# A ring of four for kept edge rows, and four operands of an attention pass in PSUM

## What is computed

```python
x = _layernorm(x + gat(x))        # layer 0: two gat_conv, 4 heads of 32
x = _layernorm(x + neighbours(x)) # layer 1: weighted sum over edges, two branches
x = _layernorm(x + attention(x))  # layer 2: 8 heads of 16, then a feed-forward
x = _layernorm(x + edge_mlp(x))   # layer 3: per-edge MLP with two batchnorms, mean

# a gat_conv: softmax over the edges of a node, then a weighted sum
e = leaky_relu(alpha_s[src] + alpha_d[dst], 0.2)
e_exp = exp(e - segment_max(e, dst)[dst])
out = segment_sum(h[src] * (e_exp / denom[dst])[:, :, None], dst)

# layer 2: the score is a product of the node's query and the edge's key
w = einsum('ehd,ehd->eh', q[dst], k[src])

# layer 3
e = (x[dst] - x[src]) @ theta_w.T + x[src] @ phi_w.T
e = relu(bn(e, bn0_g, bn0_b)) @ fc1_w.T
e = relu(bn(e, bn1_g, bn1_b))     # bn needs sums over all edges first
x = relu(segment_sum(e, dst) / max(count, 1) + x)
```

## Time and profile before

| | us |
|---|---|
| median of 3 runs | 14954.79 |
| lowest and highest run | 14942.3, 14955.02 |
| the profiled execution | 14914.23 |
| its span | 14912.4 |
| busy in it: POOL, DVE | 8357.2, 7009.2 |
| busy in it: PE, ACT | 3867.0, 2521.3 |

### The profile page before, as it was taken

One profiled execution on the slowest core, in us unless ns is written; L12 is line 12 of the kernel. 1 busy time (PEld: TensorE's weight loads), 2 busy tenths in 40 slices (PEclk: granted clock), 3 DMA queues, 4 the chain that ended last, 5 costly groups with the idle time before them and its releaser, 6 DMA issues. The chain is left out here.

```text
span 14912.4 us, 95989 instructions
## 1 busy us (share of the span) xinstructions
PE 3867.0 (26%) x15751; PEld 2525.5 (17%) x15850; DVE 7009.2 (47%) x10781; ACT 2521.3 (17%) x6154; POOL 8357.2 (56%) x7838
## 2 busy tenths in 40 slices
PE   2011122223211222326920000000421111127666
PEld 1011011222211122223420000000211111113322
DVE  8673355556444555552034555555532222234454
ACT  0411122233212223320000000000000000004454
POOL 0116777777577777770017777777157777750012
PEclk9997565666655665657955555555655555558788
DMA  0002544444336434454703633333126433344444
GB/s 2 12 27 57 69 84 90 96 96 102 68 73 83 90 90 96 101 91 165 259 26 91 96 98 98 98 98 99 16 79 91 111 105 105 104 105 159 146 171 148
DMA packets 840654, 1414.44 MB, mean 95 GB/s; under 512 B 191956, under 2 KB 623802, under 8 KB 827672
## 3 DMA queue, kind: packets, MB, share of 16 engines
q0 software_dynamic: 277856, 659.70, 22.2%
q10 hardware_dynamic: 448192, 336.76, 8.3%
q1 hardware_dynamic: 114552, 417.44, 8.1%
HBM read 1058.01 MB, written 355.29 MB: 95 GB/s over the span
## 5 line engine op out<-in xcount | busy, mean ns | idle before, releaser
L851 POOL DMA_INDIRECT ring<-gat_table,index x3640 | 4056.4, 1114 | 1172.0 <-issue 1041.1
L851 POOL DMA_INDIRECT ring<-kv_table,index x1820 | 2030.2, 1115 | 577.8 <-issue 524.3
L851 POOL DMA_INDIRECT ring<-b_table,index x1820 | 1730.9, 951 | 670.0 <-issue 516.8
L982 PE MATMUL pairs<-hot_lo,hot_hi 128*128 128x128 f32 x6272 | 949.9, 325 | 1234.2 <-ACT hot_lo L1012 1232.7
L1076 DVE TENSOR_TENSOR prod<-ring,p 128x1848 f32<-128x1848 f32 (+1 forms) x390 | 820.3, 2103 | 721.7 <-DVEq L107 682.0
L982 PEld LDWEIGHTS pairs<-hot_lo,hot_hi 128*128 128x128 f32 x6272 | 923.7, 238 | 1287.4 <-issue 1285.9
L1012 ACT ACTIVATE hot_lo<-hot_lo,wt 128x128 f32<-128x128 f32 x3136 | 934.3, 387 | 1167.5 <-remote 1009.8
L1642 DVE TENSOR_TENSOR tb<-bt,att 128x1792 f32 x130 | 263.2, 2024 | 1663.7 <-DVEq L107 1663.7
L976 PE MATMUL pairs<-nil 128*128 128x512 bf16 x686 | 341.4, 596 | 2675.6 <-ACT dstage L1021 2629.6
L1125 ACT ACTIVATE p<-x 128x84 f32<-128x84 f32 (+1 forms) x390 | 114.2, 293 | 5220.4 <-DVE x L1072 5220.4
L1664 PE MATMUL bt<-ident,ring 128*128 128x128 f32 x1820 | 417.3, 421 | 1932.1 <-PEq L107 1932.1
(11 more groups left out here) (372 smaller groups left out, 8955.0 us busy)
## 6 DMA issues: line engine op xcount, KB each, us to landing
dense_weights<-dstage ACTq DMA_DIRECT2D x196, 1024.0 KB
mat<-dense_weights SPq DMA_DIRECT2D x98, 1568.0 KB
kept<-tb ACTq DMA_DIRECT2D x132, 896.0 KB, 3.8
layer_out<-kept SPq DMA_DIRECT2D x130, 896.0 KB
at<-kept SPq DMA_DIRECT2D x130, 896.0 KB
ring<-gat_table,index POOLq DMA_INDIRECT x3640
ring<-kv_table,index POOLq DMA_INDIRECT x1820
ring<-b_table,index POOLq DMA_INDIRECT x1820
```

The source lines that it names most:

```text
L851: pool.indirect_dma_start(self.ring[:, r * UG + i, :], None, self.table, bass.IndirectOffsetOnAxis(self.index[:, half, at:at + 1], 0)).the ...
L982: mm = pe.matmul(self.ps[:, b, i * P:(i + 1) * P], self.hot_hi[:, 4 * b + i, :], self.hot_lo[:, 4 * b + i, :], start=False, stop=False, sk ...
```

## The change

- In `attention_pass` the tile `prod` of 14 rows is replaced by `first` and `second` of 7 rows each, and its instruction by two, one for each edge. The kept share gets a tile `kept_share` of its own and an ACT instruction of its own. Where `beside` is None, which is layer 2, `p`, `first` and `acc` lie in PSUM; in layer 0 all of them stay in SBUF.
- The tile `qt` of layer 2 lies in PSUM.
- `KeptUnits` has its own ring `kept_ring` of `RU` = 4 units. SP issues two loads ahead of its loop and four in a round; ACT, PE and DVE take units 0 and 1 first and then four in a round. The tile `fold` of the spread pass lies in that ring, its `own` and `prod` in `layer_out`. Own batches stand before each of the first 7 rounds of four.

```diff
@@ -1038,9 +1038,12 @@
     with ExitStack() as st:
         s = k.sub(st)
         ga = Gather(k, s, table, width, slot_src)
-        e, x, p = (s.sb(n, [P, S + 1, HW]) for n in ("e", "x", "p"))
+        e, x = (s.sb(n, [P, S + 1, HW]) for n in ("e", "x"))
+        place = s.sb if beside is not None else s.ps
+        p, kept_share = place("p", [P, S, HW]), s.sb("kept_share", [P, HW])
+        first, second = place("first", [P, B7, VB]), s.sb("second", [P, B7, VB])
+        acc = place("acc", [P, B7, VB])
         warm = s.sb("warm", [P, 1])
-        prod, acc = s.sb("prod", [P, UG, VB]), s.sb("acc", [P, B7, VB])
         rden, newmax = s.sb("rden", [P, HW]), s.sb("newmax", [P, HW])
         work = extra(s)
         ch, e_ready, p_ready = (k.sem(n) for n in ("atchain", "e_ready", "p_ready"))
@@ -1073,21 +1076,24 @@
                                   ALU.subtract).then_inc(e_ready, 1)
                 claim(dve, p_ready)
                 weight = p[:, :, :].rearrange("p s (w h) -> p (s w) h", h=heads)
-                dve.tensor_tensor(by_head(prod[:, :, :]), by_head(got[:, :, 0:VB]),
-                                  weight[:, 0:UG, :].unsqueeze(3).broadcast_to([P, UG, heads, dim + 1]),
-                                  ALU.mult).then_inc(ga.used, 1)
+                share = kept_share[:, :].rearrange("p (w h) -> p w h", h=heads)
+                for half, dst in ((0, first), (1, second)):
+                    part = slice(half * B7, (half + 1) * B7)
+                    ins = dve.tensor_tensor(by_head(dst[:, :, :]), by_head(got[:, part, 0:VB]),
+                                            weight[:, part, :].unsqueeze(3).broadcast_to([P, B7, heads, dim + 1]),
+                                            ALU.mult)
+                ins.then_inc(ga.used, 1)
                 c(dve.tensor_tensor(by_head(acc[:, :, :]), by_head(acc[:, :, :]),
-                                    weight[:, UG:UG + B7, :].unsqueeze(3).broadcast_to([P, B7, heads, dim + 1]),
-                                    ALU.mult))
-                c(dve.tensor_tensor(prod[:, 0:B7, :], prod[:, 0:B7, :], prod[:, B7:UG, :], ALU.add))
-                dve.tensor_tensor(acc[:, :, :], acc[:, :, :], prod[:, 0:B7, :], ALU.add)
+                                    share.unsqueeze(3).broadcast_to([P, B7, heads, dim + 1]), ALU.mult))
+                c(dve.tensor_tensor(second[:, :, :], first[:, :, :], second[:, :, :], ALU.add))
+                dve.tensor_tensor(acc[:, :, :], acc[:, :, :], second[:, :, :], ALU.add)
                 c.reset()
 
             if rows_of is not None:
                 parts = Running(k, dve, EROWS)
                 parts.put(rows_of.chunks(dve, 0))
             with dve.Fori(0, NB) as b:
-                start(dve, c, b * B7, acc, e[:, S, :], work, prod)
+                start(dve, c, b * B7, acc, e[:, S, :], work, second)
                 c.reset()
                 u0 = band_start(k, dve, b)
                 if rows_of is None:
@@ -1122,7 +1128,8 @@
             def exponents(n):
                 with act.Fori(0, n):
                     take(act, e_ready)
-                    act.activation(p[:, :, :], x[:, :, :], ACT.Exp)
+                    act.activation(p[:, :, :], x[:, 0:S, :], ACT.Exp)
+                    act.activation(kept_share[:, :], x[:, S, :], ACT.Exp)
 
                     act.activation(e[:, S, :], newmax[:, :], ACT.Copy).then_inc(p_ready, 1)
 
@@ -1450,7 +1457,7 @@
                           lambda row: row[:, VB:2 * VB].rearrange("p (h c) -> p h c", h=H)[:, :, C:C + 1])
 
             stw.close()
-            qt = s1.sb("qt", [P, B7, VB])
+            qt = s1.ps("qt", [P, B7, VB])
             with ExitStack() as st2:
                 block = st2.enter_context(k.block())
 
@@ -1755,37 +1762,46 @@
 
 
 
-    def __init__(self, k, s, kept, coef, slots):
-        self.k, self.kept, self.coef, self.slots = k, kept, coef, slots
+    def __init__(self, k, s, kept, coef):
+        self.k, self.kept, self.coef = k, kept, coef
+        self.slots = s.sb("kept_ring", [P, RU, S * W7])
         self.r4 = s.sb("r4", [P, 2 * S, QW])
-        self.loaded = [k.sem(f"tb{h}_in") for h in range(2)]
+        self.loaded = [k.sem(f"tb{h}_in") for h in range(RU)]
         self.tb_free, self.r4_free, self.relued = k.sem("tb_free"), k.sem("r4_free"), k.sem("relued")
 
     def few(self, eng):
         return eng.If(pairs_of_units(self.k, eng) <= CAP // 2)
 
-    def pairs(self, eng):
-        return pairs_of_units(self.k, eng, CAP // 2)
+    def rounds(self, eng):
+        return eng.value_load(self.k.total[0:1, 1:2], min_val=NB + 1, max_val=CAP // RU)
 
     def prime(self, eng):
-        eng.sem_inc(self.tb_free, 2)
+        eng.sem_inc(self.tb_free, RU)
         eng.sem_inc(self.r4_free, 2 * S)
 
     def sync(self, sp):
+        def fetch(r, unit):
+            claim(sp, self.tb_free)
+            u = unit if isinstance(unit, int) else unit.with_bounds(min_val=0, max_val=CAP - 1)
+            sp.dma_start(self.slots[:, r, :], self.kept[ds(u, 1), :, :].rearrange("g p c -> (g p) c")
+                         ).then_inc(self.loaded[r], 16)
+
         with self.few(sp):
-            with sp.Fori(0, self.pairs(sp)) as i:
-                for h in range(2):
-                    claim(sp, self.tb_free)
-                    u = (2 * i + h).with_bounds(min_val=0, max_val=CAP - 1)
-                    sp.dma_start(self.slots[:, h * S * W7:(h + 1) * S * W7],
-                                 self.kept[ds(u, 1), :, :].rearrange("g p c -> (g p) c")).then_inc(self.loaded[h], 16)
-
-    def act_unit(self, act, h):
-        claim(act, self.loaded[h], 16)
+            for r in range(2):
+                fetch(r, r)
+            with sp.Fori(0, self.rounds(sp)) as i:
+                for r in range(RU):
+                    fetch((r + 2) % RU, RU * i + r + 2)
+
+    def act_units(self, act, slots):
+        for r in slots:
+            self.act_unit(act, r)
+
+    def act_unit(self, act, r):
+        claim(act, self.loaded[r], 16)
         for q in range(2 * S):
             claim(act, self.r4_free)
-            at = h * S * W7 + q * QW
-            act.activation(self.r4[:, q, :], self.slots[:, at:at + QW], ACT.Relu,
+            act.activation(self.r4[:, q, :], self.slots[:, r, q * QW:(q + 1) * QW], ACT.Relu,
                            bias=self.coef[:, 1:2], scale=self.coef[:, 0:1]).then_inc(self.relued, 1)
 
 
@@ -1795,9 +1811,10 @@
 
     with ExitStack() as st:
         s = k.sub(st)
-        source = KeptUnits(k, s, kept, coef, flat2(k.out[:, :, :]))
-        stats, fold = s.sb("stats", [P, CAP * 2 * S, 2, 3]), s.sb("fold", [P, CAP * 2 * S, 2])
-        own, prod = s.sb("own", [P, W7]), s.sb("prod", [P, W7])
+        source = KeptUnits(k, s, kept, coef)
+        stats = s.sb("stats", [P, CAP * 2 * S, 2, 3])
+        fold = flat2(source.slots[:, :, :])[:, 0:CAP * 4 * S].rearrange("p (g h) -> p g h", h=2)
+        own, prod = (flat2(k.out[:, i * B7:(i + 1) * B7, :]) for i in range(2))
         pad_sums = s.sb("pad_sums", [P, NB, 2])
         e1, d = s.ps("e1", [P, 2 * S, 512]), s.ps("d", [P, 2, 512])
         ch, product, bank_free, own_ready, own_free, d_done, d_free = (k.sem(n) for n in (
@@ -1810,18 +1827,17 @@
         def _(act):
...
@@ -1810,18 +1827,17 @@
         def _(act):
             def own_batch(b):
                 claim(act, own_free)
-                act.activation(own[:, :], at[:, ds(b * W7, W7)], ACT.Relu, bias=coef[:, 1:2],
+                act.activation(own, at[:, ds(b * W7, W7)], ACT.Relu, bias=coef[:, 1:2],
                                scale=coef[:, 0:1]).then_inc(own_ready, 1)
 
             with source.few(act):
-                last = source.pairs(act)
+                last = source.rounds(act)
+                source.act_units(act, (0, 1))
                 with act.Fori(0, NB) as b:
                     own_batch(b)
-                    source.act_unit(act, 0)
-                    source.act_unit(act, 1)
+                    source.act_units(act, (2, 3, 0, 1))
                 with act.Fori(NB, last):
-                    source.act_unit(act, 0)
-                    source.act_unit(act, 1)
+                    source.act_units(act, (2, 3, 0, 1))
 
         @block.tensor
         def _(pe):
...
-                last = source.pairs(dve)
+                last = source.rounds(dve)
                 source.prime(dve)
                 dve.sem_inc(bank_free, 2 * S)
                 dve.sem_inc(own_free, 1)
                 dve.sem_inc(d_free, 1)
                 c(dve.memset(stats[:, :, :, :], 0.0))
                 c.reset()
+                for u in range(2):
+                    unit(u)
                 with dve.Fori(0, NB) as i:
                     own_batch(i)
-                    unit(2 * i)
-                    unit(2 * i + 1)
+                    for u in range(RU):
+                        unit(RU * i + u + 2)
                 with dve.Fori(NB, last) as i:
-                    unit(2 * i)
```

(11 more changed lines are left out.)

24 lines of the change are left out of this document (14 added, 10 removed).

## The result

The changed kernel takes 13918.24 us (median of 4 runs, 13916.23 to 13925.74), beside 14948.55 for the kernel before on the same chip (4 runs, 14920.12 to 14955.02): a ratio of 0.9315, 95% interval 0.9299 to 0.9331. I had forecast 13815, with 13720 to 13980 as the range. The profiled execution took 13925.74 us with a span of 13923.9; before it was 14912.4. Between these two executions lie 988.5 us, where I had forecast 1138; between the medians lie 1030. So a difference of some 20 us between kernels of two sets is within that spread, and is read from the profiles.

What follows compares the result with a forecast made beforehand. POOL's gathers, held by DVE instructions with two SBUF inputs, bound the attention passes; two load places bound the kept passes. 299 + 229 + 327 + 283 = 1138 us off 14914 gives 13776, as median about 13815, range 13720 to 13980.

Steps and rivals of the forecast that it cites:

- Layer 2: Layer-2 attention: with one PSUM input in the wide DVE instructions, gathers are no longer held; 299 us less, range 256 to 310.
- Rivals (3): Layer-2 attention: PSUM inputs don't free the gathers, because it is not the port; nothing gained there, 14114 us; chance 0.05.
- (4): Layer-2 attention: PSUM operands make DVE the bound and the kernel slower than before, 15090 us; chance 0.01.
- Layer 0: Layer-0 attention: stalls stay, but the divided product holds gathers for less time; 229 us less, bounds nothing to 593.
- 260 units x 0.88 us: Layer-0 attention: the third gather begins at 3012.56 instead of 3013.44, a saving taken for every unit; 229 us.
- Rival (2): Layer-0 attention: the halves hold the port as one, so nothing is gained there; 14044 us; chance 0.07.
- Spread pass: First kept pass: four places make PE the bound at 0.75 us a product; 440 us against 767, 327 less.
- Mean pass: Second kept pass: DVE the bound at 0.77 us a product; 453 us against 736, 283 less.
- lead 5: Mean pass: 5 us counted before the products, within its sum of 453 us.
- 0.5 us of slow clock each: Mean pass: added to `dve_rows`' 7.6 us at each of six changes of band, 48 us together.
- Rivals (1): Kept passes gain only part: overlapping loads slow one another or PE's clock stays low; 14075 us (0.12), in full 14425.
- (5): Kept passes: the ring does nothing, SP's loads being served one at a time; 14425 us; chance 0.02, shared with (1) in full.

Runs made afterwards that it cites:

- the two edits: Changed kernel with layer 0's five wide instructions each cut into 4 + 3 tiles of nodes and empty slots reading 128 dummy rows: 13519.39 us.
- ring alone: Kernel before with only the changes to `KeptUnits` and its users, the ring of four for kept rows: 14377.99 us, ratio 0.962.
- empty slots: Changed kernel with 128 dummy rows in each table, an empty slot of partition i reading the i-th: 13729.81 us, ratio 0.9196.
- the query alone: Changed kernel with the tile `qt` back in SBUF instead of PSUM: 14094.66 us, ratio 0.9429.

## Why the mean pass gained less

After's mean pass has 20.9 us before its first product (forecast 5), 428.0 us for 520 products, 0.823 each (forecast 0.77), and six gaps for `dve_rows` of 7.5 us or less, 43.7 together (forecast 48 with the slow clock).

**The lead** is in the timeline of its start:

```profile
13396.25 28.89 SPq L1786 DMA_DIRECT2D kept_ring<-kept  x6
13401.00 2.72 ACT L1804 ACTIVATE r<-kept_ring,coef 128x448 f32<-128x448 f32 x4 [9.29 <-ACTq L107]
13406.19 3.37 POOL L2107 TENSOR_SCALAR lift<-ext,coef,bound 128x896 f32<-128x896 f32 x1 [518.55 <-issue]
...
13414.43 2.07 POOL L2110 TENSOR_TENSOR acc<-acc,lift 128x896 f32<-128x896 f32 x1
...
13417.11 1.27 DVE L2103 SCALAR_TENSOR_TENSOR acc<-e,bound,acc 128x448 f32<-128x448 f32 x2 [22.40 <-DVEq L107]
```

ACT has its four quarters at 13403.7. DVE waits until POOL has worked out the first band's start value, at 13416.5. So I moved these four instructions to DVE, on top of the two edits:

```diff
+                    tail.first_init(dve, c)
...
-                    tail.pool_init(pool, c, 0, 0)
```

> As the kernel with both edits, and the first band's start value of the mean pass (four instructions over 896 columns) on DVE, which waits for it, instead of on POOL. In the profile of after POOL begins them at 13406.19, 10 us behind the first load, and DVE's first product waits until 13417.11. On DVE they take about 4.5 us and can begin at about 13395. If POOL's start value sets the pass's lead, DVE's first product comes some 7 us behind the first load rather than 20.9, and the time falls by 10 to 14 us, which is under what the median can tell but plain in the profile. If PE's first product (13405) or the cold TensorE clock sets it, the lead stays above 15 us.

Measured: 13498.85 us (13496.27 to 13506.28), 0.9036 [0.9023, 0.9048], 20 less than with the two edits. Its start:

```profile
12991.95 2.73 SPq L1798 DMA_DIRECT2D kept_ring<-kept  x4
12992.30 0.75 DVE L2127 TENSOR_SCALAR layer_out<-ext,coef,bound 128x896 f32<-128x896 f32 x1 [1.90 <-issue]
...
12994.93 1.09 DVE L2130 TENSOR_TENSOR acc<-acc,layer_out 128x896 f32<-128x896 f32 x1
...
13000.06 0.68 DVE L2115 SCALAR_TENSOR_TENSOR acc<-e,bound,acc 128x448 f32<-128x448 f32 x1 [4.03 <-DVEq L107]
```

The first product comes 8.1 us behind the first load instead of 20.4: 12 us, as the theory has it. The other 8 us are past its 10 to 14; the products took 425 instead of 432 us, and in three kernels with this same loop (after, ring alone, empty slots) they took 426 to 430, so that they differ by as much without a cause of this kind.

**The pitch.** DVE's timeline of after, in a stretch at DVE's own pace and in a slow one:

```profile
13471.30 2.93 DVE L2103 SCALAR_TENSOR_TENSOR acc<-e,bound,acc 128x448 f32<-128x448 f32 x4 [0.16 <-DVE acc L2103]
13474.39 2.93 DVE L2103 SCALAR_TENSOR_TENSOR acc<-e,bound,acc 128x448 f32<-128x448 f32 x4 [0.16 <-DVE acc L2103]
```

```profile
13611.46 1.27 DVE L2103 SCALAR_TENSOR_TENSOR acc<-e,bound,acc 128x448 f32<-128x448 f32 x2 [0.24 <-DVEq L107]
13612.95 0.68 DVE L2103 SCALAR_TENSOR_TENSOR acc<-e,bound,acc 128x448 f32<-128x448 f32 x1 [0.22 <-DVEq L107]
13613.79 0.68 DVE L2103 SCALAR_TENSOR_TENSOR acc<-e,bound,acc 128x448 f32<-128x448 f32 x1 [0.16 <-DVE acc L2103]
13614.71 1.27 DVE L2103 SCALAR_TENSOR_TENSOR acc<-e,bound,acc 128x448 f32<-128x448 f32 x2 [0.24 <-DVEq L107]
```

3.09 us for four in the first, 3.25 in the second, where DVE waits for PE twice in four products. I took this slow pattern for the cause of the 0.823, and the next two runs ask about it. My first theory was the turn of the four places of `r`. After with three of them in the mean pass (`source.prime(dve, 2 * S - 1)`, which primes `r4_free` with it):

> After, with three places instead of four for ACT's results in the mean pass alone (r4_free primed with 3). The mean pass took 0.823 us a product where I had forecast 0.77, partly in a steady pattern of 3.26 us for four products in which DVE waits for PE and nobody is busy all the time. If that is the turn of a place (DVE gives it, ACT fills it, PE reads it, DVE takes the product) divided by four places, a turn takes 3.1 to 3.26 us and three places give 1.03 to 1.09 us a product: 520 x 0.21 to 0.26 = 110 to 138 us more, 14030 to 14056. If the turn is shorter than 2.5 us and the pattern comes from TensorE's clock or from loads that come late, three places change under 30 us: 13918 to 13948.

Measured: 13929.47 us (13921.26 to 13934.08), 0.9325 [0.9311, 0.9339], 11 more than after. The products took 438 us. That theory fell. The next one was the PSUM banks, of which DVE lets PE have two ahead:

```diff
-                    dve.sem_inc(bank_free, 2 * S - 2)
+                    dve.sem_inc(bank_free, 2 * S - 3)
```

> After, with one credit less for the PSUM banks of the mean pass: bank_free primed with 1 instead of 2, so that PE is at most one product ahead of DVE, not two. Three places for ACT's results changed the pitch only from 0.823 to 0.842 us, so that turn was not what makes the pitch 0.82 rather than 0.77. If it is the turn of a bank (DVE begins a product, PE may begin the one two further on, and DVE gets that), a turn takes 2 x 0.815 = 1.63 us in the slow pattern and at least 1.5, and with one credit each product takes that long: 520 x 0.7 to 0.8 = 360 to 420 us more, 14280 to 14340. If a turn takes only PE's 0.75 us and two short hops, 1.0 to 1.2 us, two credits are enough and something else makes the pattern: 520 x 0.2 to 0.4 = 100 to 200 us more, 14020 to 14120.

Measured: 14370.46 us (14360.52 to 14370.48), 0.9615 [0.9596, 0.9634], 452 more, 30 above the range of the theory of the banks. Its products:

```profile
13703.05 0.68 DVE L2103 SCALAR_TENSOR_TENSOR acc<-e,bound,acc 128x448 f32<-128x448 f32 x1 [0.81 <-DVEq L107]
13704.54 0.68 DVE L2103 SCALAR_TENSOR_TENSOR acc<-e,bound,acc 128x448 f32<-128x448 f32 x1 [0.81 <-DVEq L107]
13706.13 0.68 DVE L2103 SCALAR_TENSOR_TENSOR acc<-e,bound,acc 128x448 f32<-128x448 f32 x1 [0.90 <-DVEq L107]
```

A turn of a bank, from the start of one product on DVE to that of the product which waits for it, takes 1.49 to 1.59 us. Two ahead give 0.745 to 0.795 us a product, on either side of DVE's own 0.77. So the mean pass has next to no room there. But the slow pattern has 2 x 0.815 = 1.63 us for two products, more than these turns, so that its cause stays open; the granted clock was 1.00 in it. Over the pass a product took about 1.66 us, 0.84 more than in after, which makes up 437 of the 452 us; the granted clock was 0.86 over this pass instead of 0.94, so that some of the turns were longer than these.

**Where the 28 us are.** I had asked about the wrong stretch. Of the 129 groups of four products in after, 77 take 0.772 us a product, which is the forecast. The slow pattern stands in one band, 16 groups, and another band has 13 groups at 0.783; beside 0.772 the two cost 3.3 us. In ring alone, whose products took 426 us, the 0.815 doesn't occur at all. Some 24 us stand where a band begins. DVE's rows at the first change of band, and two windows behind it (columns as above):

```profile
13510.53 0.68 DVE L2103 SCALAR_TENSOR_TENSOR acc<-e,bound,acc 128x448 f32<-128x448 f32 x1 [1.47 <-DVEq L107]
...
13521.13 1.28 DVE L2103 SCALAR_TENSOR_TENSOR acc<-e,bound,acc 128x448 f32<-128x448 f32 x2 [0.74 <-DVEq L107]
13523.45 0.68 DVE L2103 SCALAR_TENSOR_TENSOR acc<-e,bound,acc 128x448 f32<-128x448 f32 x1 [1.05 <-DVEq L107]
13525.04 2.98 DVE L2103 SCALAR_TENSOR_TENSOR acc<-e,bound,acc 128x448 f32<-128x448 f32 x4 [0.90 <-DVEq L107]
```

```profile
13521.00:13523.00 2.00, 1.82 (x3) 1.03 (x4) 1.28 (x2) 1.37 (x2) 1.92 (x2) 0.50 0.03 8
13523.00:13525.80 2.80, 2.80 (x7) 1.15 (x5) 1.36 (x2) 1.66 (x3) 2.34 (x4) 0.71 0.00 0
```

At each of the six changes DVE loses 1.4 to 1.6 us in the products ahead of `dve_rows`, and 1.6 to 2.9 us in those behind it, on top of the gap itself; the first products of the pass lose 2.4. The second part goes with the granted clock: PE was idle for 6.47 us, works at 0.50 of full clock behind that, and DVE waits for it. What the first part waits for was not taken apart.

## Why the prediction came out as it did

- **Layer 2** (299 us, got 294): right in mechanism and in size, and shown by the query alone. Rivals (3) and (4) are out.
- **Layer 0** (229, got 145; 169 beside the layer 0 of ring alone): the step "260 units x 0.88 us" was mis-sized. POOL's busy time fell by 200 us, 0.77 a unit, since not every unit meets the three instructions as the one of the earlier trace rows did. 55 of these came back as idle time (29 beside ring alone): "I expect it to stay the bound" was wrong at the end of the first band, where the landing of rows is the bound and not POOL. The sign was in the trace of before: the wait of 27.80 us. I had read "issue 1041.1" of 1172.0 idle and not asked what was in the other 131; a list of POOL's waits over 1 us would have shown it. Rival (2), halves that hold as one, is out: undividing costs 182 us.
- **Spread pass** (left at 440, got 458): the product pitch was right, 0.752 for 0.75, as were the clock in the steady part and 304 GB/s for the estimated 306. The own batch costs 8.2 us and not 6.5, since a round of four units with it takes 20.2 us and four plain units 12.0; seven of them are 12 us more. I had read it off DVE alone. The lead was 8 and not 5.
- **Mean pass** (left at 453, got 494): "lead 5" is 16 us short, of which POOL's start value is 12, though before has it too. "520 x 0.77" holds between the bands. Mis-sized is "0.5 us of slow clock each": a change of band costs some 3.6 us beside `dve_rows`, which makes 22 us in six, and the start of the pass 2.4. The slow pattern is 3 us.
- Rivals (1) and (5) would have shown loads that slow one another or wait for one another; a load takes 4.6 us with two places and with four, and a unit of the spread pass goes at PE's 3.0 us. The prediction's "up to four loads under way" is the number of places: by the estimate above it is 1.5 at a time.

The main causes of all four gains were right. The size taken from a mean over a whole group (layer 2) held within 5 us; the three others were all too large, by 135 us together in the profiles. In the kept passes the clean rows gave the steady pace right, and what was short is what stands around them: leads, batches and changes of band. The miss is 150 us by the two profiles and 108 by the medians, which moved by 1030: before's profiled execution, 14914.23, was a short one, and part of layer 0's 84 is that.

## What to carry to other kernels

Where GpSimd issues indirect gathers beside VectorE, look at a gather that begins inside a wide two-input instruction: if it ends 0.8 us after that instruction, move one input to PSUM, or, where that can't be, cut the instruction in pieces. Send padding slots to many rows, never to one. When a stage's pace is forecast from a clean row, price apart what interrupts it (the lead, each batch, each change of band, the "idle that isn't issue"), and look for a second bound at the stage's ends. And when a mean comes out above the steady pace, list where it exceeds it before testing a cause.

## What the hardware did that I had not expected

- Indirect reads of one single HBM row slow the queue: 0.50 us a packet where most slots read one row, against 0.13 when they read 128. Spreading them made the kernel 188 us faster.
- A gather that begins 0.02 to 0.04 us behind the start of a two-input VectorE instruction isn't held (129 of 129 at the fold in layer 2 of before); one that begins later in it mostly is, to 0.82 us past its end.
- Cutting VectorE instructions in two costs VectorE little, and nothing where it isn't the bound: ten instructions in place of five added 99 us to its busy time and made the kernel 197 us faster.
- PSUM as input or output costs VectorE little: 2.14 us for the 1904-column product from either memory, and 1.154 us for 952 columns written to PSUM beside 1.139 to SBUF.
- Loads of 896 KB into two places bring 165 GB/s, into three 291, into four 304, which is all that PE takes; one load lands after 4.6 us in each case.
